# Sorting each token's two expert picks through DRAM in place of 16 dense experts, in a one-core decoder layer

## What is computed

```
scores = sigmoid(x @ gate_w + gate_b); values, picks = top_k(scores, 2); values /= sum(values)
out = x + mlp(x, shared) + sum over the 2 picks of value * mlp(x, expert[pick])
mlp(x, wg, wu, wd) = (silu(x @ wg) * (x @ wu)) @ wd        # 16 experts and the shared one, inner width 64
```

## Time and profile before

| | |
|---|---|
| median of 3 runs | 1685.32 us (1680.99 to 1686.09) |
| profiled execution | 1683.33 us, span 1681.5 us |
| TensorE busy / mean granted clock | 1507.0 us (90%) / 0.986 of full |
| VectorE, ScalarE, GpSimd busy | 1161.7, 866.1, 725.5 us |

### The profile page before, as it was taken

How to read it: one execution, slowest core, us unless ns; L and a number is a source line. 1 busy time by engine, 2 the same in 40 slices (tenths; PEclk the granted TensorE clock), 3 DMA queues, 4 the chain that set the end, 5 groups by cost and what they waited for, 6 DMA issues and landing times. The chain is left out here.

```text
span 1681.5 us, 32978 instructions
## 1 busy us (share of the span) xinstructions
PE 1507.0 (90%) x11552; PEld 1231.5 (73%) x11552; DVE 1161.7 (69%) x2822; ACT 866.1 (52%) x3177; POOL 725.5 (43%) x882
## 2 busy tenths in 40 slices
PE   2889999989999898998989999998999999899966
PEld 1667777877778777777877777787777778777854
DVE  3566867777676777867677786777768677776732
ACT  3655455454554545555564555546554554655411
POOL 4543535345354534535444453544435453452411
PEclk9999999999999999999999999999999999999977
DMA  3000000000000000000000000000000000000000
GB/s 136 7 7 2 6 15 4 17 3 5 15 4 17 4 16 3 5 15 5 16 3 18 2 6 15 5 16 3 18 1 6 15 5 17 3 6 1 6 2 7
DMA packets 22229, 19.15 MB, mean 11 GB/s; under 512 B 1904, under 2 KB 20912, under 8 KB 22064
## 3 DMA queue, kind: packets, MB, share of 16 engines
q1 hardware_dynamic: 22064, 17.05, 3.2%
HBM read 12.85 MB, written 4.19 MB: 10 GB/s over the span
## 5 line engine op out<-in xcount | busy, mean ns | idle before, releaser
L1247 POOL TENSOR_TENSOR pr<-pr,ri 128x480 f32<-128x480 f32 x256 | 255.5, 999 | 497.7 <-DVE ri L959 497.7
L685 ACT ACTIVATE pr<-sE,nm 128x120 f32<-128x120 f32 x512 | 178.0, 360 | 298.3 <-DVE nm L944 298.1
L422 PE MATMUL pvb<-pT,vv 120*64 120x128 f32 x2048 | 141.8, 281 | 62.5 <-DVE pT L955 60.7
L685 ACT ACTIVATE pr<-sO,nm 128x120 f32<-128x120 f32 x512 | 178.7, 378 | 0.0
L422 PEld LDWEIGHTS pvb<-pT,vv 120*64 120x64 f32 x2048 | 110.6, 138 | 92.6 <-DVE pT L955 83.3
L1266 POOL TENSOR_TENSOR ew<-e,gw 128x512 f32<-128x512 f32 x128 | 134.6, 1052 | 100.8 <-issue 82.3
L955 DVE COPY pT<-t 120x512 f32<-120x512 f32 x256 | 164.1, 682 | 0.0
L390 PEld LDWEIGHTS sE<-kT,qT 64*128 64x128 f32 x1024 | 123.4, 187 | 50.8 <-issue 50.8
L390 PE MATMUL sE<-kT,qT 64*128 64x120 f32 x1024 | 147.0, 284 | 0.0
L390 PE MATMUL sO<-kT,qT 64*128 64x120 f32 x1024 | 147.0, 284 | 0.0
L496 PE MATMUL m<-wd,eT_s 128*128 128x128 f32 x1024 | 137.8, 290 | 2.8 <-ACT eT_s L728 2.8
(11 more groups left out here) (271 smaller groups left out, 3842.1 us busy)
## 6 DMA issues: line engine op xcount, KB each, us to landing
xt<-in_x SPq DMA_DIRECT2D x16, 256.0 KB, 3.0
out_y<-y SPq DMA_DIRECT2D x64, 64.0 KB, 1.5
cT<-in_ctxT SPq DMA_DIRECT2D x16, 240.0 KB, 3.1
hT<-in_w_k SPq DMA_DIRECT2D x1, 512.0 KB, 4.8
qT<-in_w_v SPq DMA_DIRECT2D x1, 512.0 KB, 6.0
qT<-in_w_q SPq DMA_DIRECT2D x1, 512.0 KB, 6.8
wo<-in_w_o SPq DMA_DIRECT2D x1, 512.0 KB, 7.9
qT<-in_w_g SPq DMA_DIRECT2D x1, 512.0 KB, 8.2
```

The costliest lines, as they stand in the source:

```text
L422: ins = mm(pvb[r * DK:(r + 1) * DK, (k // 2) * T:(k // 2 + 1) * T], vv[:, q, h * DK:(h + 1) * DK], pT[:, 4 * r + k // 2, :], start=True, s ...
L685: ins = f(pr[:, p % RING, r, i, :], score_banks[r][:, i * S:(i + 1) * S], ACT.Exp, bias=nm[:, p % 2, r, i:i + 1], accum_out=rsum[:, p % 2, ...
L1247: GP.tensor_tensor(pr[:, p % RING, r, :, :], pr[:, p % RING, r, :, :], ri[:, p % 2, r, :, :].to_broadcast([P, 4, S]), ALU.mult).then_inc(s ...
```

## The change

The mixture is split into stages that run in later bodies: `c` routes as before and makes `base` (2 x + shared expert); for each pair of groups (`CHUNK`, 16 tiles of picks) TensorE and VectorE work out for each pick a row of a table sorted by expert (`c_rank`, `c_slots`), and GpSimd scatters the tokens there, in DRAM, with 16 indirect DMAs (`c_scatter`). Each expert's part is filled up to whole tiles of 128, so two groups have 32 tiles. Stage `d`, two bodies after `c`, takes 16 of these tiles in four quads: SyncE loads four tiles and, for each, reads the expert's number from SBUF into a register and loads that expert's weights (`d_load`); `d_T`, `d_up`, `d_act`, `d_down`, `d_y` compute them in plain float32, and `d_store` writes them back. Stage `e`, two bodies after `d`, gathers each token's two results with 8 indirect DMAs a group (`e_gather`), adds them (`e_sum`) and normalizes. There are 22 bodies in place of 18. Expert weights are no longer held in SBUF.

The core of the diff (tile declarations, semaphore counts, some waits and the first zero fill of the DRAM tables are left out):

```diff
+CHUNK = 2 * SEQ
+QUAD = 4
+QUADS = 4
+TILES = 2 * QUADS * QUAD
+SLOTS = TILES * P
+KEEP = 5
...
-            for i in range(2, G - 1):
-                body(i + 1, i, i - 1)
-            body(None, G - 1, G - 2)
-            body(None, None, G - 1)
+        def pipeline(body):
+            def there(n):
+                return n if 0 <= n < G else None
+            for t in range(-1, G + KEEP):
+                body(there(t + 1), there(t), there(t - 1), there(t - 3), there(t - 5))
...
+            def d_load(d, i):
+                k, par = d // 2, i % 2
+                row = ((d % 2) * QUADS + i) * QUAD * P
+                if i == 0:
+                    sp.wait_ge(sem["scattered"], whole("scattered", k))
+                    sp.wait_ge(sem["expert"], upto("expert", k))
+                if i >= 2:
+                    sp.wait_ge(sem["d_down"], upto("d_down", d, i - 2))
...
+                    sp.wait_ge(sem["d_down"], upto("d_down", d - 1, i + 2))
+                sp.dma_start(xq[par][:], xs[k % 2][row:row + QUAD * P, :].rearrange("(u p) n -> p u n", p=P)).then_inc(sem[f"xq{par}_loaded"], 16)
+                for u in range(QUAD):
+                    j = ((d % 2) * QUADS + i) * QUAD + u
+                    e = sp.value_load(ei[k % 2][0:1, j:j + 1], min_val=0, max_val=E - 1)
+                    sp.dma_start(wgq[par][:, u, :], w_gu[bass.ds(e, 1)].rearrange("o p n -> p (o n)")).then_inc(sem[f"wq{par}_loaded"], 16)
+                    half = (u % 2) * I
+                    sp.dma_start(wdq[par][half:half + I, u, :], w_d[bass.ds(e, 1)].rearrange("o p n -> p (o n)")).then_inc(sem[f"wq{par}_loaded"], 16)
+            def d_store(d, i):
+                k, par = d // 2, i % 2
+                row = ((d % 2) * QUADS + i) * QUAD * P
...
+                    for q in range(SEQ):
+                        sp.wait_ge(sem[f"gath{q}"], whole(f"gath{q}", 2 * (k - 2) + 1))
+                sp.wait_ge(sem["d_out"], upto("d_out", d, i))
+                sp.dma_start(yd[k % 2][row:row + QUAD * P, :].rearrange("(u p) n -> p u n", p=P), yq[par][:]).then_inc(sem[f"yq{par}_stored"], 16)
+            def e_store(e, q):
+                sp.wait_ge(sem["ln3_out"], upto("ln3_out", e, q))
...
+                sp.dma_start(out[e * SEQ + q], y[:, q % 2, :]).then_inc(sem[f"out{q}_stored"], 16)
...
+                D, F_ = d is not None, e is not None
+                if D:
+                    d_load(d, 0)
+                    d_load(d, 1)
+                for i in range(QUADS):
+                    if F_:
+                        e_store(e, i)
+                    if D:
+                        d_store(d, i)
+                        if i + 2 < QUADS:
+                            d_load(d, i + 2)
+            pipeline(body)
...
-            def c_up(c, n):
...
+            def c_shared_down(c):
...
+                pe.wait_ge(sem["shT_sb"], upto("shT_sb", c))
+                for q in range(SEQ):
+                    ins = mm(m0[:, q * P:(q + 1) * P], sT[:, q * T:(q + 1) * T], wsd[:], start=True, stop=True)
+                ins.then_inc(sem["sh_down"], 1)
...
+            def c_rank(k):
+                pe.wait_ge(sem["picked"], upto("picked", 2 * k + 1))
+                pe.wait_ge(sem["shT_sb"], upto("shT_sb", 2 * k + 1))
+                chosen = picked[:].rearrange("p q e -> p (q e)")
+                n = CHUNK * E
+                mm(m1[:, 0:n], tri[:], chosen, start=True, stop=False, skip_group_check=True)
+                for q in range(1, CHUNK):
+                    mm(m1[:, q * E:n], onesb[:], chosen[:, 0:n - q * E], start=False, stop=False, skip_group_check=True)
+                for q in range(CHUNK):
+                    ins = mm(m1[:, n:n + E], onesb[:], picked[:, q, :], start=False, stop=(q == CHUNK - 1), skip_group_check=True)
+                ins.then_inc(sem["rank"], 1)
+            def d_T(d, i, c):
+                par, n = i % 2, 2 * d + i // 2
+                pe.wait_ge(sem[f"xq{par}_loaded"], 16 * (n + 1))
+                if i:
+                    pe.wait_ge(sem["dT_sb"], upto("dT_sb", d, i - 1))
+                elif c is not None:
+                    pe.wait_ge(sem["base"], upto("base", c))
+                else:
...
+                for u in range(QUAD):
+                    ins = turn(m0[:, u * P:(u + 1) * P], xq[par][:, u, :])
+                ins.then_inc(sem["dT"], 1)
+            def d_up(d, i, c):
+                par, n = i % 2, 2 * d + i // 2
+                pe.wait_ge(sem[f"wq{par}_loaded"], 128 * (n + 1))
+                pe.wait_ge(sem["dT_sb"], upto("dT_sb", d, i))
+                if i:
+                    pe.wait_ge(sem["d_out"], upto("d_out", d, i - 1))
...
+                elif c % 2:
+                    pe.wait_ge(sem["place"], upto("place", c // 2))
+                else:
                     pe.wait_ge(sem["shT_sb"], upto("shT_sb", c))
...
-                product(m0[:], cols_of(x2T, q * T, (q + 1) * T), cols_of(split["wg"], half, half + 512)).then_inc(sem["eg"], 1)
...
-                product(m1[:], cols_of(x2T, q * T, (q + 1) * T), cols_of(split["wu"], half, half + 512)).then_inc(sem["eu"], 1)
-            def c_act_T(c, q):
...
-                for j in range(E // 2):
-                    ins = turn((m0, m1)[j // 4][:, (j % 4) * T:(j % 4 + 1) * T], ew[:, j * P:(j + 1) * P])
...
-                        ins.then_inc(sem["eT"], 1)
-            def c_down(c, q):
...
-                for j in range(E // 2):
-                    mm(m1[:, 0:P], eT[:, j, :], wd[:, j, :], start=(j == 0), stop=False)
-                mm(m1[:, 0:P], sT[:, q * T:(q + 1) * T], wsd[:], start=False, stop=True).then_inc(sem["down"], 1)
...
+                for v in range(2):
+                    for k in range(2):
+                        for r in range(2):
+                            u = 2 * v + r
+                            ins = mm(m1[r * I:(r + 1) * I, (2 * v + k) * P:(2 * v + k + 1) * P], wgq[par][:, u, k * I:(k + 1) * I],
+                                     xqT[:, u * P:(u + 1) * P], start=True, stop=True)
+                ins.then_inc(sem["d_up"], 1)
+            def d_down(d, i):
+                par = i % 2
+                pe.wait_ge(sem["d_act"], upto("d_act", d, i))
+                for u in range(QUAD):
+                    ins = mm(m1[:, u * P:(u + 1) * P], hq[:, u // 2, :], wdq[par][:, u, :], start=True, stop=True)
+                ins.then_inc(sem["d_down"], 1)
...
-                    if C and s > 1 and not odd:
-                        c_act_T(c, s // 2 - 1)
                     if B and 0 < s < PAIRS:
                         b_scores(b, s)
+                    if D and s > 1 and odd:
+                        d_down(d, (s - 3) // 2)
+                    if D and odd and s < 9:
+                        d_T(d, (s - 1) // 2, c)
+                    if D and s > 1 and not odd:
+                        d_up(d, s // 2 - 1, c)
...
+            def d_xT(d, i):
+                act.wait_ge(sem["dT"], upto("dT", d, i))
+                if i:
+                    act.wait_ge(sem["d_up"], upto("d_up", d, i - 1))
...
+                f(xqT[:], m0[:], ACT.Copy).then_inc(sem["dT_sb"], 1)
+            def d_tanh(d, i):
+                act.wait_ge(sem["d_up"], upto("d_up", d, i))
+                if i:
+                    act.wait_ge(sem["d_down"], upto("d_down", d, i - 1))
...
+                f(hq[:], seqs(m1[:])[:, 0:4:2, :], ACT.Tanh, scale=0.5).then_inc(sem["d_tanh"], 1)
+            def d_y(d, i):
+                par, n = i % 2, 2 * d + i // 2
+                act.wait_ge(sem["d_down"], upto("d_down", d, i))
                 if n:
...
-                f(et[:], m0[:], ACT.Tanh, scale=0.5).then_inc(sem["e_tanh"], 1)
-            def c_actT(c, q):
...
-                for k, src in enumerate((m0, m1)):
...
-                    f(eT[:, 4 * k:4 * k + 4, :], seqs(src[:]), ACT.Copy).then_inc(sem["eT_sb"], 1)
...
+                    act.wait_ge(sem[f"yq{par}_stored"], 16 * n)
...
+                f(yq[par][:], seqs(m1[:]), ACT.Copy).then_inc(sem["d_out"], 1)
...
+            def c_base(c):
+                dve.wait_ge(sem["sh_down"], upto("sh_down", c))
+                if c >= KEEP:
+                    dve.wait_ge(sem["mix0"], whole("mix0", c - KEEP))
+                V.scalar_tensor_tensor(base[c % KEEP][:], x2[c % 3][:], 2.0, seqs(m0[:]), ALU.mult, ALU.add).then_inc(sem["base"], 1)
...
+            def c_slots(k):
+                n = CHUNK * E
+                V.tensor_scalar(tn[:], m1[:, n:n + E], 1.0 / P, 0.49609375, ALU.mult, ALU.add).then_inc(sem["tile_n"], 1)
+                V.tensor_copy(tf[:], tn[:]).then_inc(sem["tile_f"], 1)
+                V.tensor_tensor_scan(te[:], ones16[:], tf[:], 0.0, ALU.mult, ALU.add).then_inc(sem["tile_end"], 1)
+                V.tensor_tensor(ts[:], te[:], tf[:], ALU.subtract).then_inc(sem["tile_start"], 1)
+                V.tensor_tensor(le[:], te[:].unsqueeze(1).to_broadcast([P, TILES, E]), iota_t[:].unsqueeze(2).to_broadcast([P, TILES, E]),
```

(83 more changed lines are left out.)

313 lines of the change are left out of this document (165 added, 148 removed).

## The result

The changed kernel takes 1848.87 us (median of 4 runs, 1846.47 to 1851.68), the kernel before 1684.76 on the same chip: ratio 1.0979, 95% interval 1.0954 to 1.1003, so 9.8% slower. The profiled execution took 1846.47 us. Its page, beside the earlier trace rows: span, busy times, and TensorE's granted clock in 40 slices.

What follows compares the result with a forecast made beforehand. VectorE's queue, not TensorE, was taken as the bound: a steady body 82.3 + 4.1 + 9.7 + 4 = 100.1 us against 99.0. Span 1681.5 - 37 + 12 + 136 = 1792.5, forecast 1795, range 1670 to 1910.

Steps and rivals of the forecast that it cites:

- 82.3 us as what a body can fall to, VectorE's queue as the limit: Steady bodies: one without experts lasts 82.3 us, so the saving is capped at 16.7 a body; VectorE's work sets steps.
- What TensorE gives back: TensorE per group: 34.8 us removed, 12.3 added, so 22.5 less a body, 360 us of busy time in all.
- x: SyncE's time for a tile's register load with its arithmetic: taken as 1.2 us, bounds 0.2 and 2.5.
- Of the 6 us at quad 3 I count 4: TensorE's two 3 us waits for quad 3's late loads behind `out_y` add 4 us to a steady body.
- At 24 x 1.2 it fits, pair s being needed two steps later.: GpSimd's queue: up to 24 indirect DMAs a body at 1.2 us each fit in without lengthening it.
- Contention against cover, set to zero: Steady bodies: GpSimd slowing VectorE's operations and TensorE's work covering VectorE's additions were taken to cancel.
- The tail: 206 forecast: After attention's last product: bodies 16 to 18 at 55 us each, plus gathers and last store, 206 against 69.5 before.
- The 41 for groups 14 and 15: Bodies 19 and 20: 8 sequences gathered in double buffers at some 4.5 us each, 36, and 5 for the last store.
- The clock rival: Two TensorE waits of 3 us a body lower its clock, costing 5 us a body, 55 in all: 1850 us; chance 0.13.
- Dear registers: Rival of dear descriptors or registers: a quad at 14.2 us adds 77, about 1930, or 1900 for milder values; chance 0.15.
- The faster rival: New VectorE work falls into its waits for TensorE and register loads are short: 1632 us; chance 0.15.
- The signs: Expected in the trace: TensorE busy near 1507 - 360, bodies near 100 us, load waits, attention ending 25 earlier, tail over 190.

Runs made afterwards that it cites:

- e2: Load of the quad after next put ahead of the store of finished tiles too, on e1: 1776.99 us.
- e3: Expert of a tile made a constant, so no register loads or arithmetic on SyncE, on the changed kernel: 1835.56 us.
- e1: On SyncE each quad's store and the load of the quad after next put ahead of `out_y`, on the changed kernel: 1782.36 us.
- e5: GpSimd's gathers and scatters of a step put behind attention's layer norm and the mixer's norm, on e2: 1743.70 us.
- e6: 15 of the 16 scatters of each pair of groups left out, on e2: 1718.37 us.
- e9: Tail quad loads issued earlier, ScalarE's `d_y` ahead of `d_xT`, four gathers ahead of the first norm in groups 14 and 15, on e7: 1685.29 us.
- e8: 12 filler mask products on TensorE ahead of waits for `xq` of quads 2 and 3 and quad 3's weights, on the changed kernel: 1853.02 us.
- e11: Filler of 6 and 9 mask products on TensorE ahead of the tail's up and down products, on e10: 1662.61 us.
- e4: `c_slots` moved from ahead of pair 2's copies and maxima to behind its maxima, on the changed kernel: 1854.41 us.
- e7: `c_slots` moved behind the maxima of pair 2, as in e4, on e5: 1721.33 us.
- e10: ScalarE reads the register and issues the weights of each quad's fourth tile for groups 13 to 15, on e9: 1667.63 us.

## Why the prediction was right and wrong

Forecast 1795 us, range 1670 to 1910, slower with 0.81; measured 1848.9. Sign and range held; the forecast was 54 us low. By the marks above some 4 us of that lie in bodies 1 to 4, 33 in the later ones and 15 in the tail. By its steps:

**82.3 us as what a body can fall to, VectorE's queue as the limit.** Borne out by the sum, though no run isolates it. Bodies 1 to 4 saved 33.0, 37 forecast: body 1 took 85.3, under its 86.4, but body 2, the first with slots and scatters, 94.3, since the sum left both out there. Once the late loads are gone (e2), a body without slots takes 92.9; by the terms of the sum without SyncE and slots it is 82.3 + 4.1 + 7.6 = 94.0.

**What TensorE gives back.** Mis-sized: busy time fell by 101, not 360. Part is that the group sums of the earlier trace rows overlap. TensorE's timeline of the kernel before:

```profile
765.03 0.40 PE L257 MATMUL m<-wg_s_hi,x2T_s_lo 128*128 128x512 f32 x1
765.27 0.39 PE L255 MATMUL m<-wu_s_hi,x2T_s_hi 128*128 128x512 f32 x1
```

A record lasts 0.40 but the next starts 0.24 later, so a third of the 315.5 us for six interleaved groups is counted twice: their union is 211.8. With the other removed groups it is 445, not 557; the added work is 242, not 197. And what stayed got slower, from 1106 to 1195 us: the output product alone went from 129.9 to 162.4 us. The term was not in the sum of the time, so it cost nothing there.

**SyncE.** A quad takes 7.6 us, not 8.9: x is 0.65, not 1.2, and the two issues of a tile 1.14 (e3), not 0.94. "Of the 6 us at quad 3 I count 4" and nothing for quad 2: measured are 7 us in a body without slots and nothing in a slot body (e1), 3.0 in the mean. The mechanism, the queue behind `out_y`, was named rightly. A side count was wrong, without touching the sum: two groups have 64 expert loads, not 128 (512 in the whole trace), so by issue alone 30 us, not 60.

**GpSimd: "At 24 x 1.2 it fits, pair s being needed two steps later."** This is the step that failed. The price was nearly right (1.30 from start to start), but only `b_normal` was looked at, not `rs` and `xn`, which stand behind the indirect DMAs in the same queue and are wanted at once. In slot bodies the order costs 6 us (e5), the scatters in all 11 (e6). Half of 11 is 5.5 a body; the mean of 103.7 was only 3.6 over the forecast's 100.1, since other terms were rated a little high (92.9 against 94.0 and 3.0 against 4, above). So the mean came out nearer than its terms deserve.

**Contention against cover, set to zero.** `e_sum`'s second operation took 0.96 us at 762.39 beside `b_normal`, as it did for three of four sequences, and 0.35 in the idle tail: 0.6 us more, on the 1.2 that `e_sum` was given. No run separates what it does to the time.

**The tail: 206 forecast, 220.5 measured.** 3 x 55 for the quads was 170 (until the last `sorted_y` leaves at 1793.9). That it came so near is luck, two errors that cancel: quads cheaper, but loads in series through `out_y` (e1: 32 us). The 41 for groups 14 and 15 were 51: a sequence takes 5.0 to 6.3 us, not 4.5, as the next gather waits until its buffer is read (e9: 14 us).

**The rivals.** The clock rival's 1850 is almost the time measured, but e8 does not bear it out as the cause: a wait costs 2 us by the clock where it falls, against 2.8 priced, and yet the kernel with its clock at 0.96 is no faster. e8 adds 7.8 us of filler a body, though, so it bounds the clock's price only together with the filler's. The waits themselves went with SyncE's order (e1), and whatever the clock costs at them is inside those 7 us. Dear registers are refuted by e3 in steady bodies; of the tail they are 29 us. The faster rival failed for the changed kernel, but its condition, a mean body under 90 us, or 94.3 with a tail of cheap quads, fits what came: e11 has 92.9 and 95.1, 94.0 in the mean, a tail of 151.8, and is faster.

**The signs.** The tail over 190 us and the waits for both loads came. Attention's last product did not end 25 us earlier but 12 later, and TensorE's busy time was far from 1507 - 360.

**What stays open:** the clock's price alone, contention, what the scatters cost a slot body beside GpSimd's order, and what sets the pace of the steady bodies within that 1%.

## What to carry to other kernels

When work leaves the busiest engine, look for what the new stages put ahead of others' work in queues that seemed idle: one store of SyncE that waited for a norm, ahead of the loads, cost 7 us in each body without slots and 32 in the tail; DMA issues of GpSimd ahead of a norm of two operations cost 6 in each slot body. Price every queue by what stands behind each inserted instruction and is wanted at once, not by its sum of busy time. Issue loads ahead of stores that wait, put indirect DMAs behind small operations that others wait for, and count the tail of a deeper pipeline as its own kernel: here it was 151 of the 163 us lost, and e1 to e11 took 69 off its 220.

## What the runs showed of the hardware

An indirect DMA of 128 rows of 512 bytes occupies GpSimd for 1.00 (scatter) to 1.06 us (gather), 1.30 from start to start. A register load with its arithmetic costs SyncE 0.65 us (e3), 0.27 of it in the load's own record. A VectorE sum of two SBUF tiles took 0.96 us beside a GpSimd product and 0.35 alone. Moving the slots off VectorE's chain gained nothing with other waits in place (e4) and 22 us without them (e7), so a single experiment on a kernel with several waits in series can hide a real cost. A filler that lifts the granted clock from 0.53 to 0.84 and 0.89 went with 2 us less of a tail of 154 (e10, e11; one profile each).
